# A two-layer decoder on one core: one cast and one subtraction for both row halves of the maxima, and expert rows merged in other slots of a causal step

## The reference

```
x = x + window_attention(norm(x))        # 16 heads of 16, |i - j| <= 32
x = x + cross_attention(norm(x), ctx)    # 77 context rows, padding mask per item
x = x + top2_of_8_experts(norm(x))       # three-layer experts, softmax gate
x = x + causal_attention(norm(x))        # softmax over j <= i
x = x + cross_attention(norm(x), ctx)    # 77 context rows, one mask for all
x = x + quantised_gated_ffn(norm(x))     # whole-tensor scales, 16-bit roundings
```

## Time and profile before

| | us |
|---|---|
| median of 3 runs (lowest, highest) | 2122.26 (2119.05, 2122.82) |
| the profiled execution's own time | 2117.94 |
| its span, first to last instruction | 2116.1 |
| mean granted TensorE clock | 0.972 of full speed |
| PE busy | 1949.5 (92%) |
| DVE busy | 1256.2 (59%) |
| ACT busy | 978.8 (46%) |
| POOL busy | 685.5 (32%) |

### The profile page before, as it was taken

How to read it: one execution, slowest core, us unless ns; L and a number is a source line. 1 busy time by engine, 2 the same in 40 slices (tenths; PEclk the granted TensorE clock), 3 DMA queues, 4 the chain that set the end, 5 groups by cost and what they waited for, 6 DMA issues and landing times. The chain is left out here.

```text
span 2116.1 us, 57339 instructions
## 1 busy us (share of the span) xinstructions
PE 1949.5 (92%) x19802; PEld 1598.6 (76%) x19802; DVE 1256.2 (59%) x5456; ACT 978.8 (46%) x1905; POOL 685.5 (32%) x1244
## 2 busy tenths in 40 slices
PE   7999998999959999999999798899899998999889
PEld 5888886777748999999999577777777775444377
DVE  5788885777541111111115689988778886369964
ACT  2555555666613333333333355555566653357400
POOL 3666664356560000000001554543422320013400
PEclk9999998999969999999999899999999999999999
DMA  7333332334339999999995634433233330000023
GB/s 223 109 112 109 110 128 82 107 108 132 104 117 407 366 345 341 343 339 340 345 342 201 186 119 131 129 121 124 81 103 111 108 113 29 0 0 0 0 68 92
DMA packets 209555, 334.75 MB, mean 158 GB/s; under 512 B 59501, under 2 KB 193426, under 8 KB 200306
## 3 DMA queue, kind: packets, MB, share of 16 engines
q1 hardware_dynamic: 194914, 301.82, 41.4%
q0 software_dynamic: 9552, 26.10, 4.0%
q10 hardware_dynamic: 4928, 4.72, 0.6%
HBM read 193.74 MB, written 28.05 MB: 105 GB/s over the span
## 5 line engine op out<-in xcount | busy, mean ns | idle before, releaser
L2364 ACT ACTIVATE moe_h<-moe_h_ps,moe_weights 128x128 f32<-128x128 f32 x424 | 132.5, 363 | 255.6 <-PE moe_h_ps L2332 226.1
L2797 PE MATMUL ffn_prod_ps<-x_sb,ffn_weights 128*128 128x512 f32 x480 | 210.9, 599 | 7.0 <-ACT ffn_sig_q L2783 7.0
L2396 DVE TENSOR_TENSOR moe_y<-moe_y_ps,moe_weights 128x256 f32<-128x256 f32 x53 | 22.5, 424 | 328.2 <-PE moe_y_ps L2344 328.2
L1398 ACT ACTIVATE causal_prob<-causal_ps 128x768 f32<-128x768 f32 (+1 forms) x192 | 168.7, 878 | 79.3 <-PE causal_ps L1721 79.0
L2275 POOL DMA_DIRECT2D moe_y_dram<-moe_y x71 | 39.4, 554 | 492.5 <-DVE moe_y L2396 484.3
L2332 PE MATMUL moe_h_ps<-moe_h,moe_weights 128*128 128x128 f32 x1696 | 198.1, 275 | 0.0
L2332 PEld LDWEIGHTS moe_h_ps<-moe_h,moe_weights 128*128 128x128 f32 x1696 | 193.6, 192 | 0.1
L2797 PEld LDWEIGHTS ffn_prod_ps<-x_sb,ffn_weights 128*128 128x128 f32 x480 | 91.1, 192 | 124.6 <-issue 110.4
L1071 DVE CUSTOM_DVE_ANT_0 causal_masked<-causal_ps,causal_causal_mask 128x256 bf16<-128x256 f32 (+1 forms) x512 | 151.9, 351 | 32.0 <-PE causal_ps L1687 31.5
L1071 DVE CUSTOM_DVE_ANT_0 window_masked<-window_ps,window_window_mask 128x160 bf16<-128x160 f32 x512 | 135.1, 319 | 45.8 <-PE window_ps L1687 44.6
L1687 PE MATMUL causal_ps<-k_pair,q_pair 64*128 64x78 f32 (+2 forms) x1024 | 101.6, 299 | 35.6 <-DVE causal_m_tok L1071 26.5
(11 more groups left out here) (424 smaller groups left out, 4776.6 us busy)
## 6 DMA issues: line engine op xcount, KB each, us to landing
moe_weights<-moe_w_in SPq DMA_DIRECT2D x53, 2180.0 KB, 9.7
q_pair<-parts SPq DMA_DIRECT2D x512, 128.0 KB
parts<-moe_w_in SPq DMA_DIRECT2D x17, 2180.0 KB, 9.4
k_pair<-parts SPq DMA_DIRECT2D x256, 128.0 KB
k_pair<-parts SPq DMA_DIRECT2D x256, 38.5 KB
moe_y_dram<-moe_y POOLq DMA_DIRECT2D x71, 128.0 KB, 4.0
moe_rows<-moe_slots_dram SPq DMA_DIRECT2D x53, 128.0 KB, 3.8
x_before_ffn_dram<-x_sb SPq DMA_DIRECT2D x16, 256.0 KB, 2.1
```

The source lines that it names most:

```text
L1398: nc.scalar.activation(out, src, ACT.Exp).then_inc(expd, 1)
L2364: nc.scalar.activation(out[:, f, :], psum[:, f // 2, (f % 2) * TM:(f % 2) * TM + TM], ACT.Gelu, bias=bias[:, f:f + 1]).then_inc(done, 1)
L2797: op = nc.tensor.matmul(prod_ps[:, slot, f, :].rearrange("p (b t) -> p b t", b=2), w[:, k, at:at + P], x_cols(n // GROUPS, k), start=(k == ...
```

## The change

Two edits, both in `attention`. `split_max` reaches both row halves with one access pattern (`by_pair`: halves 64 columns apart, 4 heads, 2 token tiles), so one cast and one subtraction of 16 elements a partition take the place of two and two of 8. And from step 3 on the four merges stand in slots 2, 2, 5 and 7 in place of 4, 5, 6 and 7; steps 0 to 2 keep theirs.

```
+        MERGE_AT = (2, 2, 5, 7)
...
+                def by_pair(cols):
+
+                    return bass.AP(cols.tensor, cols.offset, [list(cols.ap[0]), [64, 2], [1, 4], [maxw, ST]])
+
...
-                    cols = m_cols[:, hf].rearrange("p s c -> p c s")
-                    for ab in range(2):
-                        op = nc.vector.tensor_copy(cols[:, 64 * ab:64 * ab + 4, :], m_tok[:, hf, ab])
-                    op.then_inc(m_hi, 1)
+                    both_halves = lambda first: by_pair(m_cols[:, hf, :, first:first + 4])
+                    nc.vector.tensor_copy(both_halves(0), m_tok[:, hf]).then_inc(m_hi, 1)
                     dve.wait_ge(m_hi, n + 1)
-                    for ab in range(2):
-                        op = nc.vector.tensor_tensor(cols[:, 64 * ab + 4:64 * ab + 8, :], m_tok[:, hf, ab],
-                                                     cols[:, 64 * ab:64 * ab + 4, :].bitcast(F32), ALU.subtract)
+                    op = nc.vector.tensor_tensor(both_halves(4), m_tok[:, hf], both_halves(0).bitcast(F32), ALU.subtract)
                     op.then_inc(m_lo, 1)
...
-                        if i >= 4 and in_merge(ref, 2):
-                            merge_rows(t + 2, ref + 2, i - 4)
+                        if in_merge(ref, 2):
+                            for n in range(4):
+                                if i == (MERGE_AT[n] if ref >= 3 else n + 4):
+                                    merge_rows(t + 2, ref + 2, n)
```

## The result

The changed kernel takes 2130.67 us in the median of 21 runs (2121.43 to 2138.02), against 2121.63 for the kernel before (21 runs on the same chip, 2111.16 to 2129.44): a ratio of 1.0043, with a 95% interval of 1.003 to 1.0056. It is slower by 0.43%, outside the range of 2105 to 2121, and the forecast was a gain. The profiled execution took 2137.44 us, near the top of its runs, and 19.5 more than the one of before.

The account below looks back on a forecast made before the run. PE's waits for DVE's causal row maxima bound the kernel, with POOL close behind. Gains of 5.9 + 1.6 + 1.9 = 9.4 us take 2117.94 to 2108.5, or 2112.9 on the runs' scale; 8 in 10: 2105 to 2121.

Parts of the forecast that it names:

- What bounds the kernel: PE waits 26.5 us for causal row maxima, about 17 in steps 3 to 12; DVE and POOL arrive together at `next_rows`.
- the 0.59 forecast: Gain per step in steps 3 to 12: 0.50 us from `next_rows` ending earlier, 0.09 from smaller waits for `row_max(0)`.
- The split: One cast and one subtraction in `split_max` save 0.18 us a split, 0.5 to 0.6 beside POOL in slot 3.
- Slots 2, 4, 6: Merges leave slots 4 and 6, two hide in slot 2's DVE idle; PE's slot 6 wait falls from 0.66 to 0.15.
- Rstd 0.20 earlier: POOL's second cut regains 0.17 us without slot 4's merge, plus 0.03 in L55, so `rstd` ends 0.20 earlier.
- The step that failed: `next_rows`' second instruction goes just ahead of POOL's unmoved third cut: 0.73 us instead of 1.05, ending about 0.5 earlier.
- The first rival: POOL holds the line: the cut still catches `next_rows`' second instruction; 2.9 us and about 1 gained, 2118.4; chance 0.23.
- The sum: 5.9 us from ten causal steps, 1.6 from the window phase's cross layer, 1.9 from other waits: 9.4 us gained.
- The window phase's cross layer: DVE is full ahead of PE's 9 waits, 3.4 us; 0.18 off each gives 1.6 us, bounds 0 and 3.4.
- The slower one: Slot 2's merges hold the gather's first DMA up to 0.87 us, deciding over 0.35; 2127.5; chance 0.10.
- DVE alone was the bound: POOL's chain shortens with DVE's load, the waits of slots 6 and 7 go: 17 us, 2101.8 in all; chance 0.12.

## Why the prediction was wrong

**What bounds the kernel.** This was right: the waits of slots 6 and 7 for the maxima, and DVE and POOL arriving together at `next_rows`. With `next_rows` out of the way the two edits gave 0.70 us a step, near the 0.59 forecast.

**The split.** Quiet, the gain was counted at 0.09 us for each pair. By source, the changed kernel's single cast and subtraction in the causal stage (ns min/median/max) are:

```profile
L1053 DVE CAST causal_m_cols<-causal_m_tok x64: 150/194/1024, 1208.6 to 1777.0; 128x16 fp32r<-128x16 f32 x64
```

```profile
L1055 DVE TENSOR_TENSOR causal_m_cols<-causal_m_tok,causal_m_cols x64: 186/200/634, 1208.8 to 1777.2; 128x16 fp32r<-128x16 f32 x64
```

0.19 and 0.20 us against 0.23 and about 0.25, so 0.09 a split and not 0.18: an instruction of 16 elements is 0.03 dearer than one of 8. Beside POOL the low part of q starts 4.76 us after the value placing began, against 5.15, with two merges now ahead of it: 0.39 earlier, where 0.5 was forecast.

**Slots 2, 4, 6.** Right. No idle before slot 3, the merges of slot 2 take 0.87 us, PE's wait of slot 6 is gone (0.15 forecast). That of slot 7, forecast near 1.0, is 1.43 even where `next_rows` meets no cut ahead of it.

**Rstd 0.20 earlier.** Wrong in sign. The second cut fell from 1.43 to 1.22 us as forecast, but the first DMA of the gather rose from 1.03 to 1.23 (1.13 to 1.29 in seven steps), and L53, now beside the merge n = 2, from 0.18 to 0.37 us. From value placing to the end of `rstd` it is 10.10 to 10.12 us in seven of the ten steps, against 9.88 to 10.03 before.

**The step that failed: "the second is issued near 1331.53, just ahead of the cut, whose start hangs on ACT and PE and stays", with `rstd` and `next_rows` 0.20 earlier.** The order of the two turned, and both sides of it had been forecast wrongly. Count from the start of the value placing in each step. `next_rows` started at 9.91 to 10.09 us; in place of 0.20 earlier it starts at 10.14 to 10.25 in seven of the ten steps, since `rstd` is late. The exponential on which the cut's start hung ended at 9.91 to 10.08; in these steps it ends at 9.59 to 9.84. So the cut waits for ACT no longer and starts, at 10.08 to 10.10, as soon as POOL is done with `rstd`, 0.06 to 0.15 ahead of `next_rows`.

Why the exponential moved stands in rows of the kernel before, step 7:

```profile
1327.65 1.14 PE L1872 MATMUL causal_psb<-causal_causal_wv,causal_xT 64*128 64x256 f32 x8
...
1330.05 0.37 PE L1721 MATMUL causal_ps<-q_pair,k_pair 64*128 64x256 f32 x4
```

```profile
1330.11 0.60 ACT L1485 ACTIVATE causal_v_stage<-causal_psb 128x512 f32<-128x512 f32 x1 [1.18 <-PE causal_psb L1872]
1330.60 0.81 ACT L1398 ACTIVATE causal_prob<-causal_ps 128x768 f32<-128x768 f32 x1
```

The exponential's matmuls (1330.05) stand ahead of PE's wait of slot 6 (to 1331.07 in the earlier trace rows), so that wait doesn't hold it. ACT's copy of v does, and the copy waits for PE's projection of v. That projection starts 0.15 to 0.18 us after DVE's low part of q ends, in all ten steps, since in the kernel it writes the PSUM tile that the low part of q reads. The low part of q is what the split makes earlier, and the prediction followed it along DVE alone. The projection starts at 6.16 to 6.31 us before. With the split alone it starts at 5.85 to 6.03 in nine steps, and in these nine the cut is ahead of `next_rows`; in the tenth, at 6.20, it isn't. With the merges alone it starts at 6.42 to 6.44 in nine steps, the exponential ends at 10.17 to 10.27, and the cut stays behind in all ten. In the changed kernel it starts at 5.85 to 6.03 in the eight steps with the cut ahead, and at 6.07 and 6.20 in the two others.

What the turned order costs shows inside the changed kernel. In the two steps in which the cut starts 0.10 and 0.14 behind `next_rows`, `next_rows` takes 1.05 us and PE's wait of slot 7 is 1.46 and 1.43. Step 5 is one of the two:

```profile
1303.45 0.45 PE L1690 MATMUL causal_ps<-k_pair,q_pair 64*128 64x256 f32 x4 [1.43 <-DVE causal_m_tok L1072]
```

In the eight others `next_rows` takes 1.27 to 1.36, where 0.73 was forecast, and the wait is 1.99 to 2.27. In one of these eight, step 3, `rstd` is not late (9.88) and the wait is still 1.99, so the collision does it without the late `rstd`. In the seven with the late `rstd`, `next_rows` ends 0.46 us later than before in the mean (11.51 against 11.05), 0.19 of it by its later start and 0.27 by its longer duration. The first rival has a collision with the cut too, but with `rstd` earlier, and so it gave a gain of 0.2 us a step. No run holds the cut back and leaves all else as it is, so the order's own price is read from these steps and from moving `next_rows`, not from a run that changes the order alone.

The Trainium skill (SBUF — State Buffer, Who interferes with whom) says that issue order decides which engine blocks when they share the port pair. By that rule, the trace agrees: an order that turned by 0.2 to 0.3 us raised the price of `next_rows` from 1.05 us to 1.27 or more and lowered that of the cut from 1.37 to 1.27.

**What the prediction lacked: the clock.** It counted PE's idle time as time and no more, so that 0.66 + 1.03 in two pieces and 1.69 in one cost the same. The changed kernel has 2.0 us in one piece in eight steps, and matmuls behind it run at the lower clock; `first_quads` at 2.2 to 2.6 us is what is seen of it. This term, put at nothing, is the larger one: without it the failed step above would have cost 0.34 us a step. Filling the wait gave back 0.99 of the 1.33 us a step.

**The sum.** The ten steps were to give 5.9 us and cost 12.9 in the profiled execution (218.5 us against 205.6 between the `next_rows` of steps 3 and 13). In the medians the loss is 9.0. Mean clocks of 0.964 to 0.970 over the 21 runs (0.970 in the fastest, 0.964 in the slowest) fit steps that fall in the clock in some executions and not in others; only one of them has a trace, so this is argued and not shown. The window phase's cross layer lost 1.3 us of its 3.4 us of waits (1.6 forecast), but its length in single executions varies by more than that: between the starts of its first and last `rstd` (L55) lie 227.3 to 232.2 us over the traces of all kernels here, 230.2 before and 230.9 with the change. So no gain of it can be shown.

**The rivals.** The slower one was right in its sign and in the row it named, the gather's first DMA above 1.2 us. But its mechanism held up POOL by 0.10 to 0.26 us, less than the 0.35 from which it decides, and the run with the merges alone, which has that hold in full, loses nothing. With L53 it made `rstd` late, which is the 0.19 us above; it is not the cause of the collision, which comes with the split alone. That this rival gave the right sign is luck. What "DVE alone was the bound" described, both waits gone, came about only once `next_rows` was moved, with 2106.51 us (2101.8 in the rival).

## What to carry to other kernels

Before counting on a gap between two engines at a shared resource, ask what sets each side of it, and follow a start that "hangs on" a third engine back to where it comes from. An instruction that the change makes earlier can release that start through two other engines: here the low part of q on DVE, PE's projection of v, ACT's copy and exponential, and then the cut. And don't add up TensorE's waits as mere time; a change that joins two short waits, or lengthens one in a dense stretch, can cost more in clock than in waiting, and filling such a wait can give back more than it costs. Where one engine is held up by another at a small instruction on the critical line, moving that instruction by one slot can be worth more than making its neighbours cheaper: here 9.3 us for the move alone and 16.2 with the edits.

## What the runs showed of the hardware

- TensorE's granted clock fell inside a stretch in which PE is 90% busy. In steps 3 to 12, by `first_quads`: behind a wait of 1.99 to 2.27 us with none in slot 6 it was slow in eight of eight steps of the changed kernel; behind 0.66 and 1.9 in nine of ten; behind 1.13 and 1.7 in ten of ten. Behind 0.66 and 1.03, as in the kernel before, or one wait of 1.29, in none of ten.
- In between it depends on the step. Behind 0.84 to 0.99 and 1.28 to 1.38, in the run with the split alone, two of eight are slow, and a third slow one stands behind 0.44 and 1.96. In the changed kernel a wait of 1.46 has 2.50 us behind it and one of 1.43 has 1.51. In the run with `rstd` early two steps have 1.51 us behind waits of 2.34 and 2.23, and one 2.79 behind a wait of 1.43. In the split with `next_rows` in slot 7 one step has 2.79 behind waits of 0.97 and 0.39.
- `next_rows`, two tensor_scalars of 256 elements, took 0.73 us alone, 1.13 when it started 0.35 us before a cut, 1.05 when 0.10 to 0.17 us before, 1.27 to 1.41 when it started 0.01 to 0.15 us after one had, and up to 2.53 in a block of four affine_selects.
- An indirect DMA's issue on POOL took 1.03 us alone and 1.13 to 1.29 when the first of two merges with both inputs in SBUF had started 0.10 to 0.25 us before it; it then ended 0.91 us after that merge did (0.86 in the run with `rstd` early). With the merge 0.02 to 0.06 us ahead it still took 1.03. The Trainium skill (SBUF — State Buffer, Who interferes with whom) has such instructions leave descriptor generation alone, and calls the reason inferred. Where the merges came second, in the earlier trace rows, the rule and the row agree; where they came first by 0.10 us or more, the measured 0.10 to 0.26 us decide against it.
